# Four chained transformer layers on one core: Q, K and V made by feature and kept on chip, row terms by matmul, the order written out, GpSimd for the setup only

## The chip, the cores and the metric
The kernel runs on one core of a Trainium2 chip. The time is the device time of one launch in microseconds (us), median over runs. Engines: TensorE (PE, its weight loads PEld), VectorE (DVE), ScalarE (ACT), GpSimd (POOL), SyncE (SP, which here only issues transfers). All arithmetic is float32 unless stated; TensorE takes a float32 matmul in two passes, which are two instructions in the profile.

## What is computed
The input is x, 32 sequences of 32 tokens with 128 features. Four layers follow one another; each sequence has its own indices (expert 0 to 15, time step, expert 0 to 7), gate score and padding mask. Cut to what matters:

```python
# L0: adapter with a 32x32 expert matrix per sequence
h = gelu(x @ down_W.T + down_b);  h = h @ expert_W[d].T + expert_b[d] + domain_emb[d]
x = LN(h @ up_W.T + up_b + x) * ln_gamma + ln_beta
# L1: adaptive norm by time step, attention of 16 heads of 8 with bias and mask, FFN
scale, shift = split(silu(sin_emb(t)) @ W_ada + b_ada)
x = LN(x) * (1 + scale) + shift
x = x + softmax(q @ k.T / sqrt(8) + bias, masked) @ v @ Wo + bo
x = x + gelu2((LN(x) * g2 + beta2) @ W1 + b1) @ W2 + b2
# L2: FFN whose matrices (128x512, 512x128) are those of the sequence's expert
r = gelu(x @ Wi[e] + bi[e]) @ Wo[e] + bo[e] + x;  x = LN(r) * gamma[e] + beta[e]
# L3: causal attention and FFN on LN(x), then the gate
x = x + g * (layer(x) - x)
```

## The kernel before
**Tiles.** 32 x 32 tokens are 8 tiles of 128 rows (4 sequences each), tokens on the partitions. A tile goes through about 70 steps. Their names appear in the texts: `down`, `expert`, `up`, `res0` (L0); `stat_a`, `rstd_a`, `norm_a`, `aff_a` (its norm), the same with `_b` for the adaptive norm; `tr_b`, `ev_b` (transposition by TensorE and its eviction); `qkv1`, scores `sc1`, `mx1`, `sub1`, `exp1`, transposition of the probabilities `pt1`, `ctx1` (probabilities by V), `cn1` (division by the sum), `ct1`, output projection `wo1`, `res1`; FFN `ff1`, `act1`, `fo1`, `res2`; the expert layer `e1`, `et`, `gelu2`, `e2`, `res3`; L3's steps end in 3, and end with `ff3`, `act3`, `fo3`, `res5`, `gate`, `store`.

**Who does what.** TensorE (L549 to L684) does the products; it writes PSUM banks of 512 floats. VectorE (L764 to L944) takes most results out of PSUM and does statistics and norms. ScalarE (L687 to L761) does exp, gelu, the reciprocal roots (Ln then Exp on 128x1) and some evictions; it loads a function table (L730, L754, L760) at each change between the exp/ln and the gelu set. GpSimd (L947 to L1033) multiplies by gains, adds shifts and biases to the residual stream (`aff_a`, `aff_e`, `xbo*`, `xb2*`), and makes the block forms for the attention: `qbd` (Q with zeros outside its own sequence), `kex` (K, zeros outside its own head) and `vbd` (V). With these, four products of 128x128 per tile give all scores of 4 sequences and 16 heads (L633), on top of a product that puts the mask into the bank (L630).

**Q, K, V.** One product gives all three with tokens on the partitions (L622). VectorE adds the bias (L874) and transposes Q and K in 32x32 blocks (L879). V has to be on other partitions for `ctx`, so it goes to DRAM and is read back four times (L537, L541):

```python
sp.dma_start(vdram[k], qkv[:, k, 2 * D:3 * D])                       # vw
sp.dma_start(vrep[h * S:(h + 1) * S, k],
             vdram[k].rearrange("(b s) d -> s b d", b=NB))           # vr, 4 times
```

**Transfers.** All are issued by SyncE in one queue, in order: after the inputs, the attention bias `fs` (256 KB a tile), the modulation vector `ada` (each sequence's row spread over 32 partitions, L519), for each sequence its expert's matrices (512 KB, L530) and its rows of bias, gamma and beta (L532), V out and back. The weight ring has 5 tiles; a transfer waits for that of the same place in the tile before, so up to four are under way.

**Order.** A planner (`plan`) simulates the steps with durations written in a table (`STEPS`) and writes one fixed order for each engine, with buffers of 3 tiles (`SLOTS`) for nearly all that lies between the steps; an engine takes its instructions in that order and waits on semaphores.

## Time and profile before

| | us |
|---|---|
| median of 3 runs (183.81 to 186.43) | 184.84 |
| span of the profiled execution | 182.4 |
| lies around the span (median less span) | 2.4 |
| busy: TensorE, VectorE, ScalarE, GpSimd | 145.1, 132.3, 111.5, 89.2 |
| mean granted TensorE clock, share of 2.4 GHz | 0.878 |

The profiled execution has no time of its own beside its span, so the median stands for it. Busy time is the union of an engine's instructions; a matmul's shown length includes its way out of the array, so the distance from one start to the next is shorter than the length. "Issue" as the releaser of a wait means that the profile shows nothing that was waited for. PEclk is the granted clock: 1.0 is 2.4 GHz, 0.5 is 1.2 GHz, a mean lies between.

### The profile page before, as it was taken

What the parts mean: (1) busy time and instruction counts of PE and PEld (TensorE: products, weight loads), DVE (VectorE), ACT (ScalarE), POOL (GpSimd) and SP (SyncE); (2) the same over time, 40 slices, a digit from 0 to 9 for tenths busy, and PEclk for the clock granted to TensorE, in tenths of its full rate; (3) what the DMA queues carried; (4) which work ended last, traced back from release to release, by engine and by line L of the source; (5) the groups of instructions that cost most, each with busy time, mean ns of one, the idle gap of its engine ahead of it and who ended that gap; (6) DMA issues with size and microseconds to landing.
All of it is one profiled execution on the core that took longest, in us unless ns stands there. A gap on an engine that the chain in (4) does not pass through costs nothing.

```text
span 182.4 us, 4942 instructions
## 1 busy us (share of the span) xinstructions
PE 145.1 (80%) x1598; PEld 111.1 (61%) x1598; DVE 132.3 (73%) x400; ACT 111.5 (61%) x273; POOL 89.2 (49%) x137
## 2 busy tenths in 40 slices
PE   7999749470746749999899878866979899998884
PEld 7478525350534548976578648446646587887673
DVE  5847755461976869586758687896799999994823
ACT  2555644030141416949999889991484866979691
POOL 1112529280626698997323344329378577444300
PEclk9955555867597987999999999997999999999999
DMA  3996576426468389859768984997963222120101
GB/s 81 325 388 256 150 198 232 119 74 174 122 160 250 68 277 321 220 169 262 235 196 254 315 297 154 203 268 204 266 174 99 61 61 63 32 61 25 32 2 43
DMA packets 23848, 31.43 MB, mean 172 GB/s; under 512 B 3382, under 2 KB 18167, under 8 KB 23824
## 3 DMA queue, kind: packets, MB, share of 16 engines
q1 hardware_dynamic: 23554, 31.06, 57.6%
q8 instruction: 13, 0.21, 0.5%
q14 instruction: 11, 0.09, 0.2%
q10 hardware_dynamic: 270, 0.07, 0.2%
HBM read 28.50 MB, written 1.57 MB: 165 GB/s over the span
## 4 chain that ended last, share of the span: by engine, by line
SPq 36%; PE 21%; DVE 17%; issue 15%; ACT 4%; DMA 3%; POOL 1%; DVEq 0%; ACTq 0%
SPq L541 10%; SPq L532 9%; SPq L530 8%; SPq L529 5%; PE bank L633 4%; PE bank L659 3%; PE bank L664 3%; SPq L519 3%; DVE nrm L863 3%; PE bank L557 2%; DMA wexp<-in_wexp 2%; PE bank L622 2%; PE bank L671 2%; DVE xt L859 1%; DVE mx L897 1%
## 5 line engine op out<-in xcount | busy, mean ns | idle before, releaser
L732 ACT ACTIVATE lnv<-mv,eps 128x1 f32<-128x1 f32 x48 | 13.9, 290 | 18.4 <-DVE mv L854 18.1
L1011 POOL TENSOR_TENSOR vbd<-vrep,tab 128x512 f32<-128x512 f32 x16 | 17.4, 1090 | 14.9 <-DMA vrep<-vdram 10.6
L1003 POOL TENSOR_TENSOR qbd<-qkt,tab 128x512 f32<-128x512 f32 x16 | 17.6, 1104 | 11.9 <-DVE qkt L879 11.1
L633 PEld LDWEIGHTS bank<-kex,qbd 128*128 128x128 f32 x128 | 21.3, 236 | 1.6 <-issue 0.7
L633 PE MATMUL bank<-kex,qbd 128*128 128x128 f32 x128 | 21.0, 319 | 0.0
L659 PE MATMUL bank<-xt,tab 128*128 128x128 f32 x128 | 18.3, 289 | 1.5 <-DVE xt L859 1.2
L754 ACT ACTIVATE hg<-bank,tab 128x128 f32<-128x128 f32 x64 | 18.0, 383 | 1.7 <-PE bank L659 1.6
L622 PE MATMUL bank<-tab,xt 128*128 128x384 f32 x32 | 17.3, 638 | 1.9 <-DVE xt L859 0.9
L659 PEld LDWEIGHTS bank<-xt,tab 128*128 128x128 f32 x128 | 16.5, 200 | 3.9 <-issue 3.3
L664 PE MATMUL bank<-tab,hg 128*128 128x128 f32 x128 | 17.4, 281 | 1.5 <-ACT hg L754 1.4
L863 DVE TENSOR_SCALAR nrm<-res,mv,rstd 128x128 f32<-128x128 f32 x40 | 17.5, 446 | 1.2 <-ACT rstd L734 1.1
L664 PEld LDWEIGHTS bank<-tab,hg 128*128 128x128 f32 x128 | 15.4, 191 | 2.8 <-issue 2.6
L730 ACT ACT_TABLE_LOAD x12 | 15.4, 1283 | 2.7 <-DVE mv L854 2.5
L743 ACT ACTIVATE sc<-sc 128x512 f32<-128x512 f32 x16 | 10.0, 623 | 9.3 <-POOL sc L1018 8.4
L557 PE MATMUL bank<-tab,res 128*128 128x128 f32 x16 | 5.2, 327 | 12.8 <-DVE res L869 12.8
L737 ACT ACTIVATE xt<-bank 128x128 f32<-128x128 f32 x16 | 4.3, 271 | 17.4 <-PE bank L557 17.4
L746 ACT ACTIVATE pt<-bank 128x512 f32<-128x512 f32 x16 | 9.5, 597 | 6.6 <-PE bank L557 6.6
L874 DVE TENSOR_TENSOR qkv<-bank,rows 128x384 f32<-128x384 f32 x16 | 8.8, 552 | 6.4 <-issue 5.6
L1018 POOL TENSOR_TENSOR sc<-sc,mx 128x512 f32<-128x512 f32 x8 | 8.4, 1052 | 8.1 <-DVE mx L897 8.1
L557 PEld LDWEIGHTS bank<-tab,res 128*128 128x128 f32 x16 | 2.4, 151 | 16.1 <-issue 15.1
L557 PE MATMUL bank<-tab,sc 128*128 128x128 f32 x64 | 11.0, 300 | 1.4 <-ACT sc L743 1.2
L647 PE MATMUL bank<-vbd,pt 128*32 128x36 f32 x512 | 7.6, 201 | 5.5 <-POOL vbd L1011 5.4
(124 smaller groups left out, 348.2 us busy)
## 6 DMA issues: line engine op xcount, KB each, us to landing
wexp<-in_wexp SPq DMA_DIRECT2D x32, 512.0 KB, 4.1
vrep<-vdram SPq DMA_DIRECT2D x64, 64.0 KB, 3.0
fm<-in_fside SPq DMA_DIRECT2D x8, 256.0 KB, 4.9
tab<-in_tab SPq DMA_DIRECT2D x2, 768.0 KB, 7.9
selv<-in_eout SPq DMA_DIRECT2D x32, 48.0 KB, 4.7
adav<-emb SPq DMA_DIRECT2D x8, 128.0 KB
vdram<-qkv SPq DMA_DIRECT2D x16, 64.0 KB, 3.3
rows<-in_rows SPq DMA_DIRECT2D x1, 768.0 KB, 6.6
```

The lines of the kernel that those rows point to most:

```text
L532: sp.dma_start(selv[b * S:(b + 1) * S, t, :], a["eout2"][bass.ds(e, 1), :].broadcast_to([S, 3 * D])).then_inc(sig, 16)
L541: sp.dma_start(vrep[h * S:(h + 1) * S, k], vdram[k].rearrange("(b s) d -> s b d", b=NB)).then_inc(sig, 16)
L557: return pe.transpose(dst, src, ident)
L622: mm = pe.matmul(ps[:, 0:3 * D], xt[:, t, :], col("wqkv" + layer), start=True, stop=True)
L633: mm = pe.matmul(ps[:, g * P:(g + 1) * P], qbd[:, k, g].rearrange("p b s -> p (b s)"), kex[:, k, g].rearrange("p h s -> p (h s)"), start=F ...
L659: mm = pe.matmul(ps[:, c * P:(c + 1) * P], col("w1" + layer, c * P, P), xt[:, t, :], start=True, stop=True)
L664: mm = pe.matmul(ps[:, 0:D], hg[:, k, c, :], col("w2" + layer, c * D, D), start=(c == 0), stop=(c == C - 1))
L730: act.preload_act_table_set("natural_log_exp_and_others")
L754: ins = act.activation(hg[:, k, c, :], bank[BANK_OF["ff" + layer, t]][:, c * P:(c + 1) * P], ACT.Gelu_apprx_sigmoid if layer == "1" else A ...
L863: ins = dve.tensor_scalar(nrm[:, t, :], stream(layer, t), mv[:, t, 0:1], rstd[:, t:t + 1], ALU.subtract, ALU.mult)
L1003: ins = pool.tensor_tensor(qbd[:, k], qkt[:, k, 0, :, None, :].broadcast_to([P, HG, NB, S]), tab[:, None, at:at + NB, None].broadcast_to([ ...
L1011: ins = pool.tensor_tensor(vbd[:, k].rearrange("p b g w -> p (b g) w")[:, :, 0:H4 * DH].rearrange("p n (h d) -> p n h d", h=H4), vrep[:, k ...
```

## The change
**Tiles and grain.** Most steps take two tiles in one instruction or one group (statistics, norms, evictions, residual sums, FFN), the adapter four (its 32 features of four tiles lie on 128 partitions); Q/K/V, the scores and the expert products stay with one. `GRAIN` says which. Every tile has buffers of its own; the expert weights have a ring of 4 tiles in place of 5, with two transfers under way at once.

**Q, K, V by feature.** `q` and `kv` take the weights as the stationary operand, so Q and K come out with features on the partitions; Q's eviction by ScalarE scales and adds its bias (`qe`), K's by VectorE adds the bias and spreads it over four head masks (`kex`). V comes from 16 small products per tile, each 32 tokens by 32 features, put on the partitions where `vbd` needs it. V's bias is added behind `ctx` (`evct`), and K, V and the modulation vector are no longer transferred. The scores are 16 products of 32 rows by 32 columns of the array, over 4 PSUM banks.

**Row terms.** Bias rows, the modulation vector (`ada`) and the expert's bias, gamma and beta (`gb`, and rows in `e1`, `e2`) are added or made by a bf16 product of a table of ones (`oh3`, one 1 per sequence and term) with the rows split in three bf16 terms, so that their sum is the float32 row. GpSimd makes these tables once, VectorE that of the modulation vector. Norms with a gain are two VectorE instructions that read gain and shift where the product left them in PSUM (`normed`).

**Moved.** `aff_a`, `aff_e`, `sub1`, `kex1`, `vbd` from GpSimd to VectorE; the copy of `e1` to ScalarE; `xbo*`, `xb2*`, `norm_a`, `norm_b`, `norm_e`, `eb`, `qkvb`, `qkt`, `qbd` are gone; `res5` and `gate` become `base` (early) and `gate`.

**Order.** Five strings give each engine's order; TensorE's also gives the bank of each step. The planner is gone. The core of the diff (lines of before with -, of after with +):

```diff
-                    sp.dma_start(adav[:, k, :], for_tokens).then_inc(sig, 16)
...
-                    sp.dma_start(wexp[:, t % W_SLOTS, b, :],
-                                 a["wexp"][bass.ds(e, 1), :, :].rearrange("o p n -> (o p) n")).then_inc(sig, 16)
-                    sp.dma_start(selv[b * S:(b + 1) * S, t, :],
-                                 a["eout2"][bass.ds(e, 1), :].broadcast_to([S, 3 * D])).then_inc(sig, 16)
-                elif name in ("vw1", "vw3"):
-                    sp.wait_ge(done["qkvb" + layer], t + 1)
-                    sp.dma_start(vdram[k], qkv[:, k, 2 * D:3 * D]).then_inc(sig, 16)
-                elif name in ("vr1", "vr3"):
-                    arrived(sp, "vw" + layer, t)
-                    for h in range(H4):
-                        sp.dma_start(vrep[h * S:(h + 1) * S, k],
-                                     vdram[k].rearrange("(b s) d -> s b d", b=NB)).then_inc(sig, 16)
...
+                    if i >= 2:
+                        sp.wait_ge(wl_landed[i % 2], 16 * (i // 2))
+                    if t >= W_SLOTS and b == 0:
+                        ready(sp, "e2", t - W_SLOTS + 1)
+                    e = sp.value_load(eidx[0:1, i:i + 1], min_val=0, max_val=E2 - 1)
+                    sp.dma_start(wexp[:, t % W_SLOTS, b, :],
+                                 a["wexp"][bass.ds(e, 1), :, :].rearrange("o p n -> (o p) n")).then_inc(wl_landed[i % 2], 16)
+                    if not late:
+                        late = True
+                        sp.dma_start(tab[:, t3:NCOL], a["tab"][:, t3:NCOL]).then_inc(loaded["tab3"], 16)
...
-                    mm = pe.matmul(ps[:, 0:3 * D], xt[:, t, :], col("wqkv" + layer), start=True, stop=True)
...
-                    pe.matmul(ps[:].rearrange("p (h s) -> p h s", h=H), ident_bf[:],
-                              masked[:, None, :].broadcast_to([P, H, S]), start=True, stop=False)
-                    for g in range(HG):
-                        mm = pe.matmul(ps[:, g * P:(g + 1) * P], qbd[:, k, g].rearrange("p b s -> p (b s)"),
-                                       kex[:, k, g].rearrange("p h s -> p (h s)"), start=False, stop=(g == HG - 1))
...
+            def add_rows(dst, t, table, lo, n, start=False):
+                return pe.matmul(dst, oh3[:, t].rearrange("k b s -> k (b s)"), table[:, lo:lo + n],
+                                 start=start, stop=False)
...
+                    pe.matmul(dst[:, 0:P], col("wqkv" + layer, D, D), xt[:, i, :], start=True, stop=True)
+                    wv = col("wqkv" + layer, 2 * D, D).rearrange("p (g h d) -> p g h d", g=HG, h=H4)
+                    for b in range(NB):
+                        for h in range(H4):
+                            mm = pe.matmul(dst[h * S:(h + 1) * S, P + b * HG * DH:P + (b + 1) * HG * DH],
+                                           xt[:, i, b * S:(b + 1) * S], wv[:, :, h, :], start=True, stop=True,
+                                           tile_position=(0, h * S))
...
+                    for g in range(HG):
+                        pe.matmul(ps[:, at + g, 0:P].rearrange("p (h s) -> p h s", h=H4), ident_bf[:],
+                                  masked[:, None, :].broadcast_to([P, H4, S]), start=True, stop=False)
+                    for b in range(NB):
+                        for g in range(HG):
+                            part = slice(g * S, (g + 1) * S)
+                            mm = pe.matmul(ps[b * S:(b + 1) * S, at + g, 0:P], qt[part, i, b * S:(b + 1) * S],
+                                           kex[part, i, :, b * S:(b + 1) * S], start=False, stop=True,
+                                           tile_position=(g * S, b * S))
...
-                    link(dve.tensor_tensor(res[:, t, :], nrm[:, t, :], adav[:, k, 0:D], ALU.mult))
-                    ins = dve.tensor_tensor(res[:, t, :], res[:, t, :], adav[:, k, D:2 * D], ALU.add)
...
-                    ins = dve.tensor_tensor(qkv[:, k, :], bank[BANK_OF["qkv" + layer, t]][:, 0:3 * D],
-                                            row("bqkv" + layer, 3 * D), ALU.add)
...
-                    ins = dve.transpose(qkt[:, k].rearrange("p j g s -> p (j g s)"), qkv[:, k, 0:2 * D])
...
+            def normed(layer, i, gain, shift):
+                ts = tiles_of("aff_" + layer, i)
+                ready(dve, "rstd_" + layer, ts[-1] + 1)
+                for n, t in enumerate(ts):
+                    ins = dve.scalar_tensor_tensor(nrm[:, t, :], res[:, t, :], mv[:, t, 0:1], gain(n), ALU.subtract,
+                                                   ALU.mult)
+                link(ins)
+                for n, t in enumerate(ts):
+                    ins = dve.scalar_tensor_tensor(res[:, t, :], nrm[:, t, :], rstd[:, t:t + 1], shift(n), ALU.mult,
+                                                   ALU.add)
+                return ins
...
+                    ins = dve.scalar_tensor_tensor(
+                        kex[:, i], bank("kv" + layer, i, P)[:, None, :].broadcast_to([P, H4, P]), bqk[:, n, 1:2],
+                        col("head_mask")[:, :, None].broadcast_to([P, H4, P]), ALU.add, ALU.mult)
...
+                    ins = dve.tensor_tensor(
+                        vbd[:, i].rearrange("p b g w -> p (b g) w")[:, :, 0:H4 * DH].rearrange("p n (h d) -> p n h d", h=H4),
+                        bank("kv" + layer, i)[:, P:2 * P].rearrange("p (n d) -> p n d", n=n)[:, :, None, :].broadcast_to(
+                            [P, n, H4, DH]),
+                        col("seq_mask")[:, None, :, None].broadcast_to([P, n, H4, DH]), ALU.mult)
...
-                    ins = dve.scalar_tensor_tensor(nrm[:, t, :], resb[:, t, :], gate[:, t:t + 1], x_in[:, t, :],
-                                                   ALU.mult, ALU.add)
...
+                        ins = dve.scalar_tensor_tensor(x_in[:, t, :], bank("wo3", i)[:, n * D:(n + 1) * D], gate[:, t:t + 1],
+                                                       res[:, t, :], ALU.mult, ALU.add)
...
+                        ins = dve.scalar_tensor_tensor(res[:, t, :], bank("fo3", i)[:, n * D:(n + 1) * D], gate[:, t:t + 1],
+                                                       x_in[:, t, :], ALU.mult, ALU.add)
...
+                    ins = act.activation(qt[:, i, :], bank("q" + layer, i, P), ACT.Identity, bias=bqs[:, n:n + 1],
+                                         scale=1.0 / math.sqrt(DH))
...
-                    link(pool.tensor_tensor(res[:, t, :], nrm[:, t, :], selv[:, t, D:2 * D], ALU.mult))
-                    ins = pool.tensor_tensor(x_in[:, t, :], res[:, t, :], selv[:, t, 2 * D:3 * D], ALU.add)
...
-                    ins = pool.tensor_tensor(qbd[:, k], qkt[:, k, 0, :, None, :].broadcast_to([P, HG, NB, S]),
-                                             tab[:, None, at:at + NB, None].broadcast_to([P, HG, NB, S]), ALU.mult)
...
-                    ins = pool.tensor_tensor(sc[:, k], sc[:, k], mx[:, t, :, None].broadcast_to([P, H, S]),
-                                             ALU.subtract)
...
+PE_ORDER = """
+w_selb.0@0 w_sel.0@2 down.0@1 down.1@4 w_emb.0@5 expert.0@6 expert.1@7 w_bi.0@2 up.0@4 up.1@0 ada.0@4 ada.1@5
...
```

In the following pieces the rows are an engine's instructions in their built order, output<-inputs and shape, with the program's buffer names (`bank` and `ps` are PSUM, `xt` the transposed tile, `tab` the table of weights).

SyncE before, from the second tile's V on its way out to the first tile's on its way back (`adav` is the modulation vector, `selv` the expert's rows, `fm` the attention bias):

```order
L537 DMA vdram<-qkv 128x128
L519 DMA adav<-emb 128x1x256
L537 DMA vdram<-qkv 128x128
L529 TENSOR_LOAD eidx
L529 ISA x2
L530 ISA
L530 DMA wexp<-in_wexp 128x1024
L532 ISA
L532 DMA selv<-in_eout 32x384
L521 DMA fm<-in_fside 128x512
L541 DMA vrep<-vdram 32x4x128 x4
```

SyncE after, from the attention bias on; TENSOR_LOAD to the weights is one sequence, 31 more follow, and behind them the stores alone:

```order
L360 DMA sc<-in_fside 128x512 x8
L370 TENSOR_LOAD eidx
L370 ISA x2
L371 ISA
L371 DMA wexp<-in_wexp 128x1024
L375 DMA tab<-in_tab 128x1536
L370 TENSOR_LOAD eidx
```

Between V's way out and its way back stand further weights, rows and the modulation vector; afterwards only the weights follow one another.

TensorE before, up to the first `ctx1` (L557 transpositions, L622 Q/K/V of a tile, L630 mask, L633 scores, L647 `ctx1`):

```order
L630 MATMUL bank<-mask_neg,ident_bf 128x512
L633 MATMUL bank<-kex,qbd 128x128 x4
L622 MATMUL bank<-tab,xt 128x384
L557 MATMUL bank<-tab,sc 128x128 x4
L630 MATMUL bank<-mask_neg,ident_bf 128x512
L633 MATMUL bank<-kex,qbd 128x128 x4
L557 MATMUL bank<-tab,res 128x128
L647 MATMUL bank<-vbd,pt 32x36 x16
```

TensorE after, around the first `ctx1` (L497 mask, L502 scores, L508 transposition of the probabilities, L457 `ada`, L470 and L523 transpositions, L517 `ctx1`, L480 K, L485 V of a tile):

```order
L502 MATMUL ps<-kex,qt 32x128 x16
L508 MATMUL ps<-tab,sc 128x128 x4
L457 MATMUL ps<-emb,oh 128x256 x2
L497 MATMUL ps<-mask_neg,ident_bf 128x128 x4
L502 MATMUL ps<-kex,qt 32x128 x16
L508 MATMUL ps<-tab,sc 128x128 x4
L470 MATMUL ps<-tab,res 128x128 x2
L517 MATMUL ps<-vbd,pt 32x36 x32
L480 MATMUL ps<-xt,tab 128x128
L485 MATMUL ps<-tab,xt 32x32 x16
L508 MATMUL ps<-tab,sc 128x128 x4
L523 MATMUL ps<-tab,qt 128x128 x2
```

The first `ctx1` is one of two tiles, stands behind both tiles' transposed probabilities, and has no transfer ahead of it; a score group is 16 small products, and K and V of a later tile are 1 and 16.

VectorE before, around the first adaptive norms (L863 norm, L868 and L869 modulation, L874 Q/K/V bias, L879 transposition of Q and K):

```order
L868 TENSOR_TENSOR res<-nrm,adav 128x128
L869 TENSOR_TENSOR res<-res,adav 128x128
L863 TENSOR_SCALAR nrm<-res,mv,rstd 128x128
L850 TENSOR_TENSOR res<-bank,x_in 128x128
L868 TENSOR_TENSOR res<-nrm,adav 128x128
L869 TENSOR_TENSOR res<-res,adav 128x128
L874 TENSOR_TENSOR qkv<-bank,rows 128x384
L853 BN_STATS bn<-res 128x6
L854 BN_AGGR mv<-bn 128x2
L879 STREAM_TRANSPOSE qkt<-qkv 128x256
```

VectorE after, around the first adaptive norms and the first K and V (L687 and L691 norm with gain and shift, L803 K's block form, L810 V's, L825 and L832 the scores' bias and maximum):

```order
L687 SCALAR_TENSOR_TENSOR nrm<-res,mv,ps 128x128 x2
L691 SCALAR_TENSOR_TENSOR res<-nrm,rstd,ps 128x128 x2
L687 SCALAR_TENSOR_TENSOR nrm<-res,mv,rows 128x128 x2
L691 SCALAR_TENSOR_TENSOR res<-nrm,rstd,rows 128x128 x2
L803 SCALAR_TENSOR_TENSOR kex<-ps,bqk,tab 128x512
L810 TENSOR_TENSOR vbd<-ps,tab 128x16x32
L803 SCALAR_TENSOR_TENSOR kex<-ps,bqk,tab 128x512
L810 TENSOR_TENSOR vbd<-ps,tab 128x16x32
L825 TENSOR_TENSOR sc<-ps,sc 128x512
L803 SCALAR_TENSOR_TENSOR kex<-ps,bqk,tab 128x512
L832 TENSOR_REDUCE mx<-sc 128x16
```

The norms of two tiles stand together and read their gains from `ps`; K's and V's forms, made by GpSimd before, stand between them and the scores.

## Rows read from the trace of the kernel before

**Rows 1.** The page, part 1: busy us (share of the span) xinstructions.
```profile
PE 145.1 (80%) x1598; PEld 111.1 (61%) x1598; DVE 132.3 (73%) x400; ACT 111.5 (61%) x273; POOL 89.2 (49%) x137
```

**Rows 2.** Windows: us, busy us of each engine, PEclk, DMA share, GB/s.
```profile
21.00:56.30 35.30, 19.12 (x70) 12.81 (x71) 20.36 (x57) 10.39 (x29) 16.80 (x24) 0.69 0.56 160
56.30:163.80 107.50, 93.41 (x1234) 72.01 (x1235) 88.21 (x247) 78.32 (x184) 63.90 (x92) 0.95 0.64 186
163.80:182.40 18.60, 13.80 (x157) 11.62 (x155) 9.13 (x33) 12.09 (x34) 3.76 (x7) 1.00 0.09 27
...
140.00:160.00 20.00, 18.87 (x272) 14.72 (x271) 19.46 (x60) 15.06 (x39) 13.09 (x21) 1.00 0.21 59
```

**Rows 3.** Waits: who for whom, us, times, longest (first two from 21.0 to 56.3).
```profile
PE bank L557 <- DVE res L869: 12.1, 4, 6.7
...
DVE res L868 <- DMA adav<-emb: 6.9, 3, 4.1
...
PE bank L647 <- POOL vbd L1011: 5.4, 2, 3.5
```

**Rows 4.** Timeline of SyncE's queue: start us, us, queue, line, transfer.
```profile
37.66 0.52 SPq L537 DMA_DIRECT2D vdram<-qkv  x1
...
46.32 3.46 SPq L532 DMA_DIRECT2D selv<-in_eout  x1
...
50.30 1.85 SPq L541 DMA_DIRECT2D vrep<-vdram  x4
```

**Rows 5.** Timeline of TensorE, two places at the 2.4 GHz level.
```profile
61.30 0.88 PE L622 MATMUL bank<-tab,xt 128*128 128x384 f32 x2
62.02 0.38 PE L630 MATMUL bank<-mask_neg,ident_bf 128*128 128x512 bf16 x1
62.23 1.05 PE L633 MATMUL bank<-kex,qbd 128*128 128x128 f32 x8
63.12 0.27 PE L557 MATMUL bank<-tab,cx 128*128 128x128 f32 x1
63.23 0.27 PE L557 MATMUL bank<-tab,nrm 128*128 128x128 f32 x1
65.42 0.47 PE L647 MATMUL bank<-vbd,pt 128*32 128x36 f32 x32 [1.92 <-POOL vbd L1011]
65.82 0.38 PE L655 MATMUL bank<-tab,cxt 128*128 128x128 f32 x1
...
103.60 1.08 PE L681 MATMUL bank<-wexp,hg 128*32 128x128 f32 x32
104.50 1.04 PE L671 MATMUL bank<-wexp,xt 128*32 128x512 f32 x8
105.35 1.06 PE L681 MATMUL bank<-wexp,hg 128*32 128x128 f32 x32
```

**Rows 6.** VectorE's groups (busy us, mean ns; second: ns min/median/max).
```profile
L863 DVE TENSOR_SCALAR nrm<-res,mv,rstd 128x128 f32<-128x128 f32 x40 | 17.5, 446 | 1.2 <-ACT rstd L734 1.1
...
L874 DVE TENSOR_TENSOR qkv<-bank,rows 128x384 f32<-128x384 f32 x16 | 8.8, 552 | 6.4 <-issue 5.6 <-PE bank L622 0.8
...
L863 DVE TENSOR_SCALAR nrm<-res,mv,rstd x40: 304/340/1080, 16.0 to 174.0; 128x128 f32<-128x128 f32 x40
```

**Rows 7.** Timeline of ScalarE, a table load.
```profile
103.71 1.28 ACT L730 ACT_TABLE_LOAD   x1
105.01 0.29 ACT L732 ACTIVATE lnv<-mv,eps 128x1 f32<-128x1 f32 x1
```

**Rows 8.** Timeline of VectorE: first res0, last sub3, last gate.
```profile
13.04 0.29 DVE L850 TENSOR_TENSOR res<-bank,x_in 128x128 f32<-128x128 f32 x1 [0.44 <-PE bank L609]
...
163.77 0.69 DVE L889 TENSOR_TENSOR sc<-bank,mx 128x512 f32<-128x512 f32 x1
...
180.07 0.35 DVE L942 SCALAR_TENSOR_TENSOR nrm<-resb,gate,x_in 128x128 f32<-128x128 f32 x1
```

**Rows 9.** Line L530, the expert weights.
```profile
DMA to landing us min/median/max: 3.3/4.1/8.1
```

1192 lines of the change are left out of this document (544 added, 648 removed), and 4 rows, old and new, of the table DRAIN.

## The prediction
> **What bounds the kernel now.** I read the page's shares first. TensorE is busy 80% of the span, VectorE 73%, ScalarE 61%, GpSimd 49% [rows 1]: no engine is full, and four take part in each tile's chain. The stretches come next [rows 2]. From 21.0 us (the first transposition of a tile) to 56.3 us (the first product of probabilities with V) TensorE is busy 19.1 of 35.3 us and VectorE 20.4, and the granted clock is 0.69, so most of these matmuls ran at 1.2 GHz. From 56.3 to 163.8 us TensorE is busy 93.4 of 107.5 us and VectorE 88.2, clock 0.95. The last 18.6 us are one chain.
>
> The list of waits says what the poor stretch waited for: TensorE 12.1 us for `aff_b`'s result on VectorE, and VectorE in turn 6.9 us for the transfer of the modulation vector [rows 3]. The queue shows why. SyncE issues all these transfers in one row with the expert weights; one issue of an expert's rows holds it for 3.46 us, and the first V, sent out at 37.66, is asked back only at 50.30, 12.6 us later [rows 4]. So the first 56 us are bound by SyncE's queue, the 107 us after by TensorE and VectorE together.
>
> **What the change makes of the queue.** V is made by product straight into the layout that the block form needs, the modulation vector and an expert's rows become products with a table of ones: SyncE keeps the loads, the expert weights and the stores, none of which has to wait for a result except a weight's ring slot. All of GpSimd's work per tile goes too, and with it the GpSimd links of the chain.
>
> **TensorE, step by step, at 2.4 GHz.** I take the pitch, start to start, since a matmul's shown length contains its tail. From [rows 5]: Q, K and V at once 0.72 us; the mask 0.21; the four score products 0.89 (8 passes of 128 columns, 0.11 each, which is also the price of the hidden layers' four products); the 32 column-tiled passes of `ctx` 0.40; the 32 of `e2` 0.90; the 8 of `e1` 0.85; one transposition 0.11. A tile has Q/K/V and scores twice: 16 x 0.72 = 11.5, scores with mask 16 x 1.10 = 17.6, 152 transpositions 16.7, `ctx` 16 x 0.40 = 6.4, hidden layers 32 x 0.89 = 28.5, output projections 16 x 0.22 = 3.5, `e1` and `e2` 8 x 1.75 = 14.0. Sum 98.2 us.
>
> After: Q and K are two 0.22 products, V is 32 column-tiled passes like `ctx`: 0.84 in place of 0.72, +1.9. The rows added by product are 40 of 128 columns, 8 of 512 and 16 of 256 in bf16; at the mask's 0.21 for 512 that is +5.5. The scores are now 32 small passes in place of 8 large. No row of this kernel shows the new form (32 rows by 32 columns at 16 places). The low end is the 0.40 of `ctx`'s 32 passes, the high end 32 x 0.11 = 3.5 if they run one by one; I take the 0.90 of `e2`, which has 128 columns too: +0.2. Sum 106 us. Of it 10.5 us lie in the last chain (9 hidden groups, 2 `ctx`, 1 group of transpositions, 3 projections, 6 single ones), so 95.5 us are for the middle.
>
> **VectorE.** The means times counts of all its groups (the costliest two kinds stand in [rows 6]; the other figures here are from the same table) make 150 us before, the page says 132.3 [rows 1]: instructions overlap, the factor is 0.88. Changes: the Q/K/V bias and the 32x32 transposition of Q/K go (8.8 + 7.0); K's block form goes from 8 on VectorE to 16 at some 0.70 and V's form comes, 16 at 0.68, +16; `sub1` comes, 8 x 0.68, +5.4; the copy of `e1` goes to ScalarE and the expert bias to a product, -11.0. The 48 normalisations at 0.446 and the modulation (0.382 + 0.484) become 24 at 0.34 and 48 two-step ones at 0.35 (`gate`'s length undisturbed [rows 8]): -3.4, and aff_a and aff_e of GpSimd are in it. Pairs of tiles in one instruction (evictions 24 x 0.40 to 12 x 0.53, residual sums, `cn`): -10.6. The rest (base, gate, setup) is +1.2. Sum: 132, times 0.88 = 116 us busy.
>
> The 0.34 is the undisturbed length: beside a GpSimd instruction the same normalisation takes up to 1.08 us, and its mean is 0.446 against a median of 0.34 [rows 6]. GpSimd's setup (about 13 us by its own rates, over by some 25 us) may still hold a few instructions of the start by up to 1 us each.
>
> **ScalarE.** 31 table loads become 23, -10.3; 48 pairs of `rstd` become 24, -11.8; hidden activations in 256 columns, -5.5; Q's eviction +4.6, `e1`'s copy +4.8, the rest -3.1: 111.5 to 90. It bounds nothing. A table load costs 1.28 us and the next instruction starts 0.02 us behind its end [rows 7]. The Trainium skill (ScalarE: Activation LUTs, What ACT_TABLE_LOAD costs) gives about 2.66 us a switch, with a drain behind the load. By that the 8 fewer would be worth 21 us of ScalarE; these rows show no drain, so my sum has 10.3, and as ScalarE is covered either way the time is the same.
>
> **The sum.** Start: `res0` of tile 0 begins at 13.04 now [rows 8]; afterwards `up` has four tiles and stands behind a table product that needs a late load, so I put 14.5. VectorE then has 8.5 us of work in its new order up to the first `aff_b` of two tiles: first transposition at 23 (21.0 now). End: the last `sub3` to the last `gate` takes 180.4 - 163.8 = 16.6 us [rows 8] and keeps its links: 16.6 again.
>
> Middle: between 56.3 and 163.8 the kernel before did 98.2 - 9.8 (done earlier) - 10.5 = 77.9 us of pitch work in 107.5, a density of 0.725. Of the missing 29.6, 5.4 us are TensorE's wait for GpSimd's V [rows 3], about 5 the time at 1.2 GHz (clock 0.95), 14 in all are idle, the rest tails of single matmuls before a wait. Without GpSimd's wait, half the clock's and a third of the tails (groups now hold two tiles) some 19 us would stay on 77.9: 0.80 to 0.82. I take 0.82: 95.5 / 0.82 = 116.5. VectorE has 116 less 8 (setup), 8.5 (up to `aff_b`) and 8.5 (the last chain) = 91 us in the same stretch, 78%: it fits beside, and is the second bound. Span 23 + 116.5 + 16.6 = 156.1 us. The profiled span is 182.4 and the median of the three runs 184.84, 2.4 us lie around it: 158.5. So the forecast is 158 us.
>
> Both ends: at the old density, 95.5 / 0.725 = 131.7, the time is 173.7. At 0.93, which is where VectorE's 91 us fill 98% of the middle (it reached 19.46 of 20 us from 140 to 160 [rows 2]), 102.7 and the time is 144.7. The scores' low end takes 16 x 0.5 / 0.82 = 10 us off TensorE's part.
>
> **Rivals.**
> 1. Dense middle, 147 us. For it: 8 tiles' buffers instead of rings of 3, no transfer in the chain. Against: two engines of almost equal work, each in a fixed order, wait for each other.
> 2. Density as before, 173 us. For it: the order is fixed and written for durations that the chip may not keep; the early part ran at 1.2 GHz for lack of work and may again.
> 3. The weights decide, 172 us. The ring has 4 slots in place of 5, and two transfers are under way at once where there were up to four. The first `e2` stands at a third of TensorE's work, about 64 us, and tile 4's weights start there. At 4.1 us each [rows 9] a tile takes 8.2 and tile 7 is there at 97, before its turn at about 112. At the slowest landing seen, 8.1, it comes at 129, and the end some 14 us later than forecast. Against: V's, the modulation's and the experts' rows' transfers, which share the 16 engines with the weights now, are gone.
> 4. Slower, 209 us: the small score products run one by one. 3.5 us in place of 0.90, 16 times, is +42 on TensorE: 137 / 0.82 = 167, span 207. It decides from about +1.35 us a group on (21.5 us in all). For it: four in a row have the same 32 output partitions, and only the four column places are seen overlapping in this trace ([rows 5]: 32 x 0.11 would be 3.5, `e2` takes 0.90). Against: each of the four writes a bank of its own.
>
> Rival 4 has a page beside it. The Trainium skill (TensorEngine Tiling (Array Packing), Gotcha 1: PSUM Pressure) says different row tiles cannot use one PSUM bank at the same time; the four banks meet it, no run shows it. The same page (Key Properties) says that a change of tiling mode drains the array, which speaks against this change, as V and the scores add some 64 changes. In this trace a full product starts 0.07 us before the shown end of `ctx`, so no drain is seen [rows 5]; were each change to wait out a pass's tail, 0.16 us (the scores are shown 1.05 long at a pitch of 0.89), that would be 10 us of TensorE and 12 of time, inside the range.
>
> That the change doesn't do what it says is excluded by the built order: GpSimd has 17 instructions after the constants, none in a tile's chain.
>
> **Chances.** Forecast (density 0.77 to 0.87, 152 to 167 us) 0.48; rival 1 0.22; rival 2 0.13; rival 3 0.05; rival 4 0.07; no gain because stalls of several kinds add up to the old time 0.05. A measurement of this kernel tells about 2% from no change. Faster by over 2%: 0.88; within 2%: 0.05; slower: 0.07. The range 141 to 177 leaves out rival 4, the case without gain and a little of the dense end.
>
> **What would show it.** Right: the first `ctx` before 40 us in place of 56.3; TensorE idle under 15 us between the first transposition and the last `sub3`; VectorE near 116 us busy with the `norm` form at 0.34; 32 score passes within 1.1 us; the last chain 15 to 18 us. Wrong: score groups over 2 us (rival 4); waits of `e1` for the weights (rival 3); a granted clock under 0.8 past 40 us or waits of TensorE and VectorE for each other over 25 us (rival 2).

## The result: faster by 2.9%, 21 us short of the forecast

The changed kernel takes 179.44 us in the median of four runs (179.01 to 180.01), the kernel before 184.71 on the same chip: ratio 0.971, 95% interval 0.965 to 0.977. The forecast was 158 us, its range 141 to 177. The profiled execution took 179.0 us with a span of 176.3. Executions of one kernel lie 1 to 7 us apart, and those of e3_pool, e6_vact, e8_mask2 and e9_tail2 that were profiled are slow ones, more than 1.5% above the fastest of the same kernel.

### The profile after

The page's first part and, of the second, the rows of TensorE, VectorE and the granted clock (tenths in 40 slices of 4.4 us):

```profile
span 176.3 us, 6271 instructions
PE 138.0 (78%) x2582; PEld 101.3 (57%) x2582; DVE 118.7 (67%) x340; ACT 93.9 (53%) x188; POOL 15.5 (9%) x22
...
PE   7919800198786499999987889999999869776893
...
DVE  3625469978998979074965697638846998645611
...
PEclk9999999999999879999999999999999999996699
```

The busy times are those forecast: VectorE 118.7 (116 forecast), ScalarE 93.9 (90), GpSimd 15.5. TensorE is busy for less time than before ([rows 1]: 145.1) and the span is shorter by only 6 us. Windows cut at the first transposition of a tile, at the first hidden layer `ff1` and at the last `sub3` show where the time is:

```profile
core 0: us, PE busy (x) PEld busy (x) DVE busy (x) ACT busy (x) POOL busy (x), PEclk, DMA share, GB/s
0.00:34.16 34.16, 16.95 (x162) 10.11 (x163) 20.22 (x69) 9.68 (x19) 15.52 (x22) 1.00 0.81 247
34.16:61.41 27.25, 20.22 (x532) 15.06 (x533) 24.50 (x66) 10.55 (x27) 0.00 (x0) 0.99 0.69 211
61.41:152.90 91.49, 83.66 (x1672) 62.09 (x1672) 64.64 (x176) 65.47 (x124) 0.00 (x0) 0.99 0.33 96
152.90:176.30 23.40, 17.14 (x219) 14.06 (x218) 9.32 (x31) 8.20 (x19) 0.00 (x0) 0.85 0.06 18
```

The start is 34.2 us, where 23 were forecast and 21.0 stood before. From there to 61.4 us VectorE is the fuller engine (24.5 of 27.3 us, TensorE 20.2). From 61.4 to 152.9 us it is TensorE (83.7 of 91.5), VectorE has 65. Against [rows 2] the program has two parts that differ in their fullest engine.

The clock of 1.00 in the first row is not to be trusted. The trace of this execution has clock records only from 40.2 us on, and the view counts what lies before them as full speed. The products say otherwise: the four passes of `w_sel` take 3.78 us here and 1.98 in e4_start, whose trace has a recorded clock of 1.00 at that place.

```profile
5.28 3.78 PE L403 MATMUL ps<-pt,oh 17*128 17x512 f32 x4
```
```profile
4.85 1.98 PE L403 MATMUL ps<-pt,oh 17*128 17x512 f32 x4
```

The two passes of K likewise take 0.77 us at 35.4 us and 0.49 at 40.4. So this execution too was at 1.2 GHz up to 40 us, and its mean clock (0.97) stands too high.

What the start waits for stands in the list of waits:

```profile
engine line waited for: us in total, times, longest us
...
POOL bqs L901 <- DMA bqk<-in_rows: 11.9, 1, 11.9
PE ps L470 <- DVE res L691: 11.7, 1, 11.7
...
ACT xt L642 <- PE ps L523: 7.3, 6, 2.8
DVE res L867 <- PE ps L542: 7.1, 4, 4.2
DVE sc L825 <- PE ps L502: 6.7, 4, 4.4
```

TensorE's 11.7 us before its first transposition are again a wait for `aff_b`. The 12.1 us in [rows 3] lay behind the first transposition, these lie ahead of it. The waits for the modulation's transfer and for GpSimd's V, the other two of that group, are gone. GpSimd's first setup step sits 11.9 us behind two transfers of 1 KB, the Q and K biases. The timeline of GpSimd (POOL) and VectorE (DVE) shows what follows. Columns: start us, us, engine, line, operation.

```profile
12.81 0.23 POOL L901 TENSOR_SCALAR bqs<-bqk 128x2 f32<-128x2 f32 x1 [11.89 <-DMA bqk<-in_rows]
...
20.03 1.14 POOL L886 TENSOR_TENSOR brow<-kex,brow 32x512 bf16<-32x512 f32 x1
...
22.55 1.26 POOL L907 TENSOR_TENSOR x_in<-x_in,rows 128x512 f32<-128x512 f32 x1
...
24.77 1.87 POOL L884 TENSOR_TENSOR erow<-erow,ex 64x896 f32<-64x896 f32 x1
...
27.70 1.87 POOL L886 TENSOR_TENSOR ex<-erow,ex 32x896 bf16<-32x896 f32 x1
```
```profile
20.11 0.69 DVE L765 TENSOR_TENSOR res<-ps,x_in 128x512 f32<-128x512 f32 x1 [2.20 <-PE ps L451]
...
23.92 0.69 DVE L765 TENSOR_TENSOR res<-ps,x_in 128x512 f32<-128x512 f32 x1 [1.66 <-POOL x_in L907]
24.53 2.26 DVE L687 SCALAR_TENSOR_TENSOR nrm<-res,mv,rows 128x128 f32<-128x128 f32 x2
26.82 2.90 DVE L691 SCALAR_TENSOR_TENSOR res<-nrm,rstd,rows 128x128 f32<-128x128 f32 x2
29.65 0.60 DVE L687 SCALAR_TENSOR_TENSOR nrm<-res,mv,rows 128x128 f32<-128x128 f32 x2
```

Three losses: the first `res0` comes at 20.11 us in place of 14.5; the second waits 1.66 us for GpSimd's `xub.1`, which stood behind row tables and masks; and two pairs of VectorE take 2.26 and 2.90 us where the next pair takes 0.60, for just as long as GpSimd makes the row table `ex3`. That is 5.6 + 1.7 + 4.0 = 11.3 us, as much as the whole excess. e4_start below, without the second and the third, takes 9.2 us from the first `res0` to the first transposition, where this kernel takes 14.1 and 8.5 were forecast.

TensorE about 65 us, at the full clock, with the new score form (L502) in it:

```profile
64.67 0.39 PE L497 MATMUL ps<-mask_neg,ident_bf 128*128 128x128 bf16 x4
64.98 0.50 PE L502 MATMUL ps<-kex,qt 32*32 32x128 f32 x32
65.41 0.49 PE L480 MATMUL ps<-xt,tab 128*128 128x128 f32 x2
```

32 score passes take 0.43 us of pitch (64.98 to 65.41), where I took 0.90, with full products right before and behind. The four mask passes ahead of them take 0.31. In e8_mask2, which has eight, they take 0.55, so four more cost 0.24, and some 0.09 of the 0.31 belong to the change from full to small products.

```profile
88.59 0.62 PE L497 MATMUL ps<-mask_neg,ident_bf 128*128 128x128 bf16 x8
89.14 0.50 PE L502 MATMUL ps<-kex,qt 32*32 32x128 f32 x32
```

### The profile page after: what moved, and what is told of

It is laid out like the page before. It is cut to its first block, busy times and chain, and to the rows that moved or that the text cites. A ratio compares the mean times of both kernels' runs of the same rounds, so it can differ in the third digit from the quotient of the medians.

```text
span 176.3 us, 6271 instructions
## 1 busy us (share of the span) xinstructions
PE 138.0 (78%) x2582; PEld 101.3 (57%) x2582; DVE 118.7 (67%) x340; ACT 93.9 (53%) x188; POOL 15.5 (9%) x22
## 4 chain that ended last, share of the span: by engine, by line
PE 51%; DVE 21%; issue 7%; ACT 7%; SPq 5%; DMA 4%; POOL 3%; DVEq 0%; POOLq 0%
PE ps L534 9%; PE ps L542 8%; PE ps L561 5%; DMA kex<-in_rows 4%; PE ps L550 4%; PE ps L390 3%; PE ps L485 3%; DVE nrm L687 3%; DVE bn L770 3%; DVE res L691 3%; PE ps L480 2%; PE ps L508 2%; PE ps L470 2%; PE ps L529 2%; PE ps L475 2%
## 5 line engine op out<-in xcount | busy, mean ns | idle before, releaser
L534 PE MATMUL ps<-xt,tab 128*128 128x256 f32 x64 | 18.4, 439 | 1.6 <-DVE xt L787 1.3
L620 ACT ACTIVATE lnv<-mv,eps 128x2 f32<-128x2 f32 x24 | 7.0, 293 | 22.6 <-DVE mv L773 22.3
L542 PE MATMUL ps<-tab,pt 128*128 128x128 f32 x128 | 16.8, 281 | 0.0
L534 PEld LDWEIGHTS ps<-xt,tab 128*128 128x128 f32 x64 | 13.7, 225 | 4.2 <-issue 2.2
L542 PEld LDWEIGHTS ps<-tab,pt 128*128 128x128 f32 x128 | 15.6, 192 | 0.2
L803 DVE SCALAR_TENSOR_TENSOR kex<-ps,bqk,tab 128x512 f32<-128x512 f32 x16 | 11.9, 745 | 3.3 <-PE ps L485 3.3
L649 ACT ACTIVATE pt<-ps,tab 128x256 f32<-128x256 f32 x32 | 12.5, 477 | 1.5 <-PE ps L534 1.3
L470 PE MATMUL ps<-tab,res 128*128 128x128 f32 x16 | 3.7, 320 | 11.7 <-DVE res L691 11.7
L639 ACT ACTIVATE pt<-ps 128x512 f32<-128x512 f32 x16 | 9.4, 594 | 4.2 <-PE ps L508 4.1
L810 DVE TENSOR_TENSOR vbd<-ps,tab 128x512 f32<-128x512 f32 x16 | 10.7, 678 | 0.3 <-PE ps L485 0.3
L508 PE MATMUL ps<-tab,sc 128*128 128x128 f32 x64 | 9.6, 278 | 0.5 <-ACT sc L636 0.5
L825 DVE TENSOR_TENSOR sc<-ps,sc 128x512 f32<-128x512 f32 x8 | 5.5, 683 | 6.7 <-PE ps L502 6.7
L485 PE MATMUL ps<-tab,xt 128*32 128x32 f32 x512 | 8.2, 204 | 1.8 <-issue 1.8
L770 DVE BATCH_NORM_STATS2 bn<-res 128x6 f32<-128x128 f32 x40 | 9.5, 279 | 0.2
L470 PEld LDWEIGHTS ps<-tab,res 128*128 128x128 f32 x16 | 2.1, 160 | 12.9 <-issue 12.6
L480 PE MATMUL ps<-xt,tab 128*128 128x128 f32 x32 | 7.6, 321 | 2.2 <-DVE xt L787 1.6
```

The costliest lines, as they stand in the source:

```text
L480: pe.matmul(dst[:, 0:P], col("wqkv" + layer, D, D), xt[:, i, :], start=True, stop=True)
L485: mm = pe.matmul(dst[h * S:(h + 1) * S, P + b * HG * DH:P + (b + 1) * HG * DH], xt[:, i, b * S:(b + 1) * S], wv[:, :, h, :], start=True, s ...
L508: mm = pe.transpose(dst[:, g * P:(g + 1) * P], sc[:, i, g * H4:(g + 1) * H4, :].rearrange("p h s -> p (h s)"), ident)
L534: mm = pe.matmul(ps[:, BANK_OF[name, i] + c // 2, (c % 2) * 2 * P:(c % 2 + 1) * 2 * P], col("w1" + layer, c * P, P), tok, start=True, stop ...
L542: mm = pe.matmul(y, hg[:, i, c, n * P:(n + 1) * P], col("w2" + layer, c * D, D), start=False, stop=(c == C - 1))
L649: ins = act.activation(hg[:, i, c, :], ps[:, at + c // 2, (c % 2) * 2 * P:(c % 2 + 1) * 2 * P], ACT.Gelu_apprx_sigmoid if layer == "1" els ...
```

## The experiments

Times are medians of 4 runs or more. Seven runs of the kernel before stand beside each; they have medians of 184.0 to 185.9 us. Places in the table are of the profiled execution of each kernel: first transposition of a tile, first `ff1`, first `e1`, last `sub3`, and from there to the end of the last `gate`.

| kernel | transp. | ff1 | e1 | last sub3 | last chain | time |
|---|---|---|---|---|---|---|
| changed | 34.2 | 61.4 | 73.3 | 152.9 | 21.2 | 179.4 |
| e12_again | 33.4 | 60.3 | 72.6 | 155.5 | 20.9 | 179.8 |
| e1_wbis | 30.5 | 62.3 | 74.3 | 153.1 | 20.6 | 180.2 |
| e2_xt | 35.5 | 64.1 | 75.7 | 155.3 | 21.0 | 180.8 |
| e3_pool | 34.8 | 63.9 | 75.9 | 156.8 | 20.2 | 180.5 |
| e4_start | 30.0 | 60.8 | 73.3 | 153.7 | 20.9 | 178.5 |
| e5_start2 | 27.3 | 55.7 | 70.0 | 153.0 | 20.3 | 177.7 |
| e10_warm | 35.4 | 63.2 | 75.3 | 155.5 | 19.8 | 178.9 |
| e18_late | 27.9 | 56.2 | 70.5 | 150.4 | 19.8 | 174.1 |
| e17_early | 27.6 | 54.8 | 67.5 | 147.0 | 21.4 | 171.7 |
| e14_comb | 28.0 | 54.1 | 66.8 | 146.1 | 19.8 | 170.5 |
| e13_comb | 27.4 | 52.7 | 65.4 | 146.1 | 19.5 | 170.3 |

changed and e12_again are one kernel. Their last `sub3` lie 2.6 us apart, so a smaller difference between two rows tells nothing until the traces show where it comes from.

### One cause of the start at a time

**e1_wbis**, GpSimd's operations on `ex3` held back:

```diff
 elif name == "w_bis":
     ready(pool, "w_bic", 1)
+    ready(pool, "sub1", 4)
```

> The edit: GpSimd's four operations on ex3 (24.77 to 29.57 us in the changed kernel) wait until the fourth sub1 is done, about 50 us; nothing is left out. Theory S (the start is long by stalls that add up, and what follows is TensorE work that shifts with it): VectorE's two pairs at 24.53 and 26.82 (2.26 and 2.90 us) take 0.60 each, the first transposition of a tile comes at 30.2 instead of 34.2 us, and the time falls by about 4 us, to 175.5 (ratio to the kernel before 0.950). Rival M (the time is set in the middle or by the weights, and the start is absorbed): the transposition comes earlier, but the last sub3 stays at 153 us and the time at 179. Rival X (the two slow pairs are not due to GpSimd): both the pairs and the time stay as they are. If GpSimd's operations then hold VectorE's between 50 and 60 us, up to 4 us come back there.

Measured: 180.21 us, ratio to the kernel before 0.979 (0.969 to 0.988). The hold is GpSimd's: where it no longer runs the pairs take 0.60 us, and it holds VectorE again where it runs now.

```profile
24.76 0.60 DVE L687 SCALAR_TENSOR_TENSOR nrm<-res,mv,rows 128x128 f32<-128x128 f32 x2
25.40 0.61 DVE L691 SCALAR_TENSOR_TENSOR res<-nrm,rstd,rows 128x128 f32<-128x128 f32 x2
...
51.19 3.02 DVE L687 SCALAR_TENSOR_TENSOR nrm<-res,mv,rows 128x128 f32<-128x128 f32 x2
54.25 2.18 DVE L691 SCALAR_TENSOR_TENSOR res<-nrm,rstd,rows 128x128 f32<-128x128 f32 x2
```
```profile
51.19 1.89 POOL L884 TENSOR_TENSOR erow<-erow,ex 64x896 f32<-64x896 f32 x1
53.14 0.92 POOL L885 CAST ex<-erow 64x896 bf16<-64x896 f32 x1
54.14 1.87 POOL L886 TENSOR_TENSOR ex<-erow,ex 32x896 bf16<-32x896 f32 x1
```

Rival X is out. The transposition came 3.7 us earlier, as theory S has it, and the last `sub3` stayed at 153.1, as rival M has it. That does not decide for M: the two pairs at 51 us take 5.2 us in place of 1.2, so the 4.0 us came back there, and TensorE is at a granted clock of 0.50 from 55.0 to 65.2 us, where the changed kernel is for 3.4 us.

**e2_xt**, the second half of `xt` requested earlier:

```diff
 sp.dma_start(xt[:, 0:4]...)
+sp.dma_start(xt[:, 4:NT]...)
 sp.dma_start(x_in[:], ...)
```

> The edit: the transfer of the second half of xt is issued right behind the first, ahead of x, rows and the ada table. The second down product then no longer waits 3.8 us to 13.43. Theory S with the start's legs in parallel: w_emb's sum on VectorE comes some 2 us earlier (from 15.2 to 13), the first res0 moves from 20.1 to 18, but the second res0 still waits for GpSimd's xub.1 (22.55, 1.26) and the two slow pairs stay, so the first transposition stays within 0.5 us of 34.2 and the time within 1 us of 179.4. If xt_rest alone decides the start, the transposition comes at 31 and the time is 176.

Measured: 180.82 us (0.981, 0.974 to 0.987). No gain, and not for my reason alone: `w_emb`'s sum on VectorE came at 16.7 us, not at 13, since the table it needs now arrives later. GpSimd's wait for `bqk` grew too, from 11.9 to 13.3 us. Here the loads share one pace, and what is put ahead delays the rest.

**e3_pool**, GpSimd's order "w_adb w_oh3 xub.0 xub.1 w_bqs w_pre w_rows w_neg w_bis", with `w_bqs` the scaling that waits for `bqk`.

> The edit: on GpSimd the scaling of the Q bias, which waits for bqk to 12.81 us, is a step of its own behind both xub, and xub.1 comes ahead of the row tables and the masks. Theory S: xub.1 is done before 15 us, the second res0 comes at 22.3 instead of 23.92, VectorE's idle time of 1.66 us goes, and the first transposition comes 1.7 us earlier, at 32.5, the time 1 to 2 us lower, 178. If more of the start hung on that queue (w_emb's sum waits for GpSimd's ada_b), up to 3 us. Rival M: the transposition moves, the time does not.

Measured: 180.50 us (0.972, 0.962 to 0.982). The second `res0` follows the first with no wait, but the first came at 22.0 us (20.1): the one wait became another, as a cast on VectorE (L750, 0.33 us before) took 1.81 us beside the two `xub`.

**e4_start**, these three together, with `w_emb` and `w_bi` moved on TensorE.

> The three edits together, and on TensorE the product w_emb ahead of the second down and w_bi (four passes that took 3.5 us) behind both up; the copy of w_bi's result on ScalarE behind the second rstd_a. Theory S: the stalls add: the first res0 at 16.5 (20.1), no wait for xub.1, pairs of 0.60, so the first transposition at 25 us instead of 34.2; the middle stays 118 us, the last sub3 comes at 144 and the time is 170.5 us (ratio to the kernel before 0.923). Rival M: the last sub3 at 150 or later and the time 176 or more, since the weights (e2.0 frees the first slot) or VectorE between 25 and 60 take up the gain.

Measured: 178.54 us (0.968, 0.961 to 0.975). The transposition at 30.0, not 25, since the transfers set it: TensorE's `w_emb` waits 8.7 us for its table, to 15.9. Of these 4.2 us nothing is left at the last `sub3` against the row of the changed kernel, and 1.8 against that of e12_again. Again two pairs of VectorE are held at 51 us (3.8 us for 1.2), and the clock is 0.50 from 55.4 to 65.5 us.

**e5_start2**, the start written anew; the new heads of the orders:

```diff
 PE_ORDER = """
-w_selb.0@0 w_sel.0@2 down.0@1 down.1@4 w_emb.0@5 expert.0@6 expert.1@7 w_bi.0@2 up.0@4 up.1@0 ada.0@4
+w_selb.0@0 w_sel.0@2 down.0@1 expert.0@6 up.0@4 down.1@0 expert.1@1 up.1@0 w_emb.0@4 w_bi.0@6 ada.0@4
 DVE_ORDER = """
-w_oh0.0 w_ang.0 w_sbc.0 w_oh2.0 w_selc.0 w_embc.0 ebias.0 ebias.1 res0.0 stat_a.0 stat_a.1 res0.1 aff_a.0
+w_oh0.0 w_ang.0 w_sbc.0 w_oh2.0 w_selc.0 ebias.0 res0.0 stat_a.0 stat_a.1 ebias.1 res0.1 w_embc.0 aff_a.0
```

> The edit: the start written so that no leg waits for another. TensorE does the first unit's down, expert and up before the second unit's, then w_emb and w_bi; VectorE does the first res0 and its statistics before the second ebias, and w_embc behind the second res0; GpSimd does both xub first and the Q bias apart; ex3's casts go to ScalarE and its two differences to VectorE between 60 and 70 us, where VectorE has waits, instead of to GpSimd. Theory D (VectorE bounds the program up to about 61 us, TensorE from there): in the two runs with a shorter start the first ff1 came at 60.8 and 62.3 us whatever the start, since VectorE was held again by GpSimd at 50 us (3.8 us instead of 1.2). Without that hold the first transposition comes at 26 us and the first ff1 at 54 instead of 61.4, and the time is 173 (ratio 0.940). Theory C (the granted clock gives it back: a TensorE that waits more falls to half clock, and ff1 then takes 3.6 instead of 2 us): the first ff1 at 55 to 57, the last sub3 at 150 and the time at 177.

Measured: 177.72 us (175.57 to 178.44), no interval. Here the start's gain does reach the first `ff1` (5.7 us earlier); at the first `e1` 3.3 us of it are left, and at the last `sub3` nothing against the changed kernel. A part is lost at 95 to 100 us:

```profile
90.00:95.00 5.00, 3.29 (x76) 2.75 (x75) 2.79 (x6) 4.01 (x7) 0.00 (x0) 0.92 0.60 200
95.00:100.00 5.00, 4.70 (x15) 3.80 (x15) 2.83 (x10) 2.97 (x5) 0.00 (x0) 0.50 0.62 179
```

TensorE is busy 4.70 of 5 us with 15 instructions, at a granted clock of 0.50: the 1.2 GHz level in the densest part of the program. The hidden layer there takes 3.75 us in place of 1.97. TensorE had waited 1.71 us from 92.1 on, in the middle of a V group, for nothing that the profile shows:

```profile
93.81 0.44 PE L485 MATMUL ps<-tab,xt 128*32 128x32 f32 x26 [1.71 <-issue]
```

But the trace of e12_again, the unaltered kernel, has the same fall at 98 us: from the first `e1` to the last `sub3` it takes 82.9 us and e5_start2 83.0, where the changed kernel takes 79.6. The fall costs some 3 us and does not come with the short start. Against e12_again the 6.1 us of the start are 4.6 at the first `ff1`, 2.6 at the first `e1` and 2.4 at the last `sub3`. What is lost is lost ahead of the first `e1`, where e5_start2 is at a clock of 0.50 for 6.8 us (53.3 to 60.1) and e12_again for 3.4.

### What bounds the two halves

**e8_mask2** doubles the mask passes of the scores. **e11_norows** leaves the row products out, and with them the biases. The edit of e8_mask2, cut:

```diff
-for g in range(HG):
-    pe.matmul(... ident_bf ... start=True, stop=False)
+for g in range(2 * HG):
+    pe.matmul(... ident_bf ... start=True, stop=g < HG)
```

> The edit: each of the 64 bf16 mask passes of the scores is done twice (the second starts the sum anew, the result is the same): 64 passes more, 0.08 us each. Theory D: the last twelve score steps lie where TensorE bounds (past 60 us), so the last sub3 comes 12 x 4 x 0.08 = 3.7 us later and the time is 183; the four before cost little. Rival (TensorE has as much slack as its idle time, or the end hangs on VectorE or the weights): under 1.5 us, time 180.5.

> Left out: the row products of wo1, wo3, fo1, fo3, e1 and e2, that is all biases that the change adds by products there (48 passes, 32 with 0.06 us of pitch by 128 columns, 8 of 0.3, 8 of 0.07). Theory D (past 61 us TensorE bounds, and its work shifts the end one for one): 40 of the 48 lie past 61 us, 4.7 us in all, so the last sub3 comes 4 us earlier and the time is 175. Rival (the end hangs on VectorE, ScalarE or the weights): under 1.5 us.

Measured: 182.38 us (181.04 to 185.89) and 175.33 us (174.22 to 179.07; ratio 0.954, 0.937 to 0.970). From the first `ff1` to the last `sub3` it is 94.6 us with 48 passes more and 88.2 without the rows, against 91.5: +3.1 (3.7 expected) and -3.3 (4 expected). The expected sizes were too high. At the pitch in these traces e8_mask2's 48 passes are 2.7 us (0.056 each). The 35 row products of that stretch are 4.9 us, of which 16 are the last full product ahead of small ones; the 0.09 us for that change stays without them, so some 3.4 us go (my estimate from these rows). changed, e1_wbis, e2_xt, e7_tail and e10_warm, with the same work there and no fall of the clock in its midst, take 90.7 to 92.3 us, so both runs lie outside. The waits agree: past 61 us VectorE waits 21.9 us for TensorE, and TensorE 3.7 for VectorE. So there TensorE's work is the time, about one for one. The profiled execution of e8_mask2 is the longest of its four (185.9 us; the others 181.0 to 183.0). The other 5 us of its later end came ahead of `ff1` (66.6), with a granted clock of 0.66 and 0.80 from 55 to 65 us.

**e16_nosub** takes VectorE's work away in the first half:

> Left out: the eight mx1 and sub1 (the first attention's maximum and its subtraction), 1.2 us a tile on VectorE; its softmax is then taken without the maximum. Theory D (VectorE bounds from 34 to 61 us): the first four tiles' 4.8 us come off, the first ff1 at 57 to 58 instead of 61; past it TensorE bounds and the other four tiles bring nothing: the time 3 to 4 us lower, 176. Rival (the chain of one tile or TensorE bounds there): the first ff1 at 60 or later, time 179.

Measured: 180.27 us, but 176.2 to 182.6 over four runs, no interval. In the profiled execution the first `ff1` began at 59.4 from a transposition at 33.6: 25.8 us in place of 27.3. 1.1 to 1.5 of the 4.8 us came through, as e12_again has 26.9; once these eight operations are gone VectorE waits for TensorE in turn (1.16 us before `res1`). That is nearer to the rival (59.4 us; 57 to 58 under theory D, 60 or later under the rival): VectorE is the fullest engine there, but it isn't shown to be the limit. In the changed kernel's stretch VectorE waits 2.4 us for TensorE and TensorE 3.4 for VectorE. The time stays open.

**e6_vact** sends `vbd1` to ScalarE, four operations of 0.28 us each a tile:

> The edit: the eight vbd1 (0.60 us each on VectorE) go to ScalarE, four operations each with the sequence mask as scale, in the part where ScalarE is busy for 10 of 26 us. Theory D: from 34 to 60 us VectorE is what bounds (23.1 busy of 25.8), so four to six of them taken away there (2.4 to 3.6 us) bring the first ff1 from 61.4 to 58.5 us, and the time to 176.5. Rival: TensorE or ScalarE's chain decides there too, or the mask operations on ScalarE take over 1.2 us a tile and sit ahead of qe1 and exp1: no change or 1 us slower.

Measured: 183.25 us (181.72 to 185.19), slower than the unaltered kernel on the same chip (178.81 to 181.08). VectorE's relief brought nothing: ScalarE's 1.13 us per tile sit ahead of `exp1` (first one at 46.9 us, 44.0 in the changed kernel), and in the profiled execution, the longest of five, the first `ff1` slipped to 67.2 us. A moved operation counts by its place in the chain.

### The last chain

**e7_tail** and **e9_tail2** reorder it; e9_tail2's TensorE order ends with `wo3.3` ahead of `tr_g.2`:

```diff
-sc3.7@4 fo3.1@0 ctx3.2@2 pt3.6@3 pt3.7@1 ct3.2@4 wo3.2@5 ctx3.3@6 ct3.3@7 tr_g.2@0 wo3.3@2 ff3.2@4
+sc3.7@4 ctx3.2@2 fo3.1@0 pt3.6@3 pt3.7@1 ct3.2@4 wo3.2@5 ctx3.3@6 ct3.3@7 wo3.3@2 tr_g.2@0 ff3.2@4
```

> The edit: in the last chain TensorE does the third ctx3 and the last two pt3 around fo3.1, the fourth ctx3 before wo3.2, and VectorE the last cn3 before base.2 and stat_g.2 (it stood 1.7 us behind them). Theory T (the last chain is 21.2 us instead of 16.6 by its order): from the last sub3 to the end 18.5 to 19, time 177. Rival (it is 21.2 since ff3.2 runs at half clock, 3.6 instead of 2.0 us, and two tile pairs end together): 20.5 to 21, time 179.

> The edit: the last chain again, with what the first attempt showed: the fourth wo3 no longer stands behind the third tr_g (which waited 2.0 us for norm_g), the last cn3 comes before base.2, the last res4 and its statistics before ev_g.2, and the last evct3 ahead of rstd_g.2. Theory T (order): 18.5 us from the last sub3 to the last gate instead of 20.6, time 177.5. Theory C (ff3.2 at half clock, 3.6 instead of 2.0 us, is the larger part): 20 us, time 179.

Measured: 180.43 us (179.86 to 186.57) and 181.42 us (178.57 to 183.09; 0.975, 0.960 to 0.991), last chain 22.6 and 21.5 us. Theory T falls: the chain did not get shorter. `ff3.2` took 3.62 and 3.65 us, at half clock in both.

### The granted clock

**e12_again** is the unaltered kernel, **e10_warm** adds products of zeros where TensorE waits:

```diff
+for _ in range(FILL.get((name, i), 0)):
+    pe.matmul(dst[:, 0:P], idle_bf[:], idle_bf[:], start=True, stop=True)
```

> The changed kernel unaltered, on the same chip as the three that follow, so that differences of 1 to 2 us can be read against it. Expected 179.4 us, within 1 us. Theory C says that its granted clock differs from one execution to the next (0.865 to 0.971 so far) with little change of the time, since TensorE at half clock before 35 us waits for VectorE anyway, and that only a fall past 50 us costs.

> The edit: 196 bf16 products of zeros (0.08 to 0.11 us each) on TensorE in front of the steps that it waited for (30 before the second down, 90 before the first tr_b, 51 at seven places from 41 to 60 us, 42 at six places of the last chain), written into the bank that the step uses next. Theory C (waits bring the half clock, and the half clock costs what ff1.0 and ff3.2 show, 3.6 instead of 2.0 us each): the clock stays full through 55 to 66 and 160 to 167 us, and the time falls by 2 to 4 us, to 176. Rival: the falls come back elsewhere in the dense part or the fillers delay the steps behind them: within 1 us of the unaltered kernel, or slower.

Measured: 179.81 us (0.976, 0.965 to 0.987) and 178.89 us (0.972, 0.961 to 0.983). The clock of e10_warm is 1.00 in every stretch from 45 to 170 us and the last chain is 1.1 us shorter; the whole is 0.9 us better, below what two such medians can tell. e12_again's four executions took 179.5, 180.1 and 181.1 us at a mean clock of 0.875 to 0.885 and 178.8 at 0.981. That is no measure of what half clock ahead of 35 us costs: the changed kernel's trace, with a mean of 0.97, was at half clock there too, as its products showed. The next four kernels put fillers onto the short start. The first two have 183 and 186 fillers, from 22 us on, and differ in the last chain, in its order and its fillers:

> The edit: the start written anew (as in the run of that name), the last chain reordered, and fillers on TensorE only at the waits from 22 us on and in the last chain (more of them there). Theory D with C (start, dense part and last chain add once the clock does not fall): first ff1 at 55.7, dense part 91.5, so the last sub3 at 147.5; last chain 18 us; span 167, time 170 us (ratio 0.92). Rival (the program's middle has a length of its own, set by VectorE or the weights): last sub3 at 151 or later, time 175 or more.

> The same without the reordered last chain. Last sub3 at 147.5, last chain 19.2 us as in the run with fillers, time 171.5 us. If the reordered chain is worth nothing, the two runs agree within 0.5 us.

Measured: **170.29 us** (169.66 to 171.58), ratio 0.926 (0.917 to 0.934), and 170.51 us, 0.927 (0.919 to 0.934). The page of e13_comb:

```profile
PE 145.7 (87%) x2765; PEld 108.4 (65%) x2765; DVE 118.1 (70%) x342; ACT 95.3 (57%) x190; POOL 10.3 (6%) x18
...
PEclk9999999999999999999999999999999999999999
```

The clock records of this trace begin at 27.2 us; ahead of that its four `w_sel` passes take 3.78 us, so the row is right from the seventh slice on.

The last chain gave 19.5 us, not the 18 expected, and as much without its new order (19.8): that order is worth nothing. Against e10_warm, with fillers as well, e14_comb has its transposition 7.4 us earlier, its last `sub3` 9.4 us and its median 8.4 us: with fillers the start counts one for one or better. Which fillers do it:

> The shortened start with fillers at eight waits from 22 to 56 us only (109 products of zeros). Theory C (a TensorE that waits in that stretch loses the full clock at about 50 to 60 us, and once more some 35 to 40 us later, in the dense part): no half clock from 45 us up to the last chain, the last sub3 at 146 to 147 us, the last chain 20.5 us, time 172. Rival (those of the last chain bring it): the last sub3 at 150 or later, time 176.

> The shortened start with fillers at six waits of the last chain only. Theory C: half clock at about 55 us and in most executions once more between 90 and 105, the last sub3 at 150 to 153, the last chain 19.3 us, time 176. Rival: the last sub3 at 147 and the time 171.

Measured: 171.65 us (0.925, 0.916 to 0.934) and 174.06 us (0.935, 0.921 to 0.949). The early ones carry most of it. The windows of e17_early over its first half, its dense part and its last chain:

```profile
27.62:54.82 27.20, 24.35 (x611) 19.33 (x612) 24.15 (x66) 10.55 (x27) 0.00 (x0) 0.88 0.70 209
54.82:146.96 92.14, 82.82 (x1673) 60.97 (x1672) 66.84 (x179) 66.07 (x125) 0.00 (x0) 1.00 0.35 112
146.96:170.60 23.64, 17.26 (x219) 14.13 (x217) 9.33 (x31) 8.19 (x19) 0.00 (x0) 0.86 0.06 17
```

Its dense part, first `ff1` to last `sub3`, is 92.1 us at clock 1.00. e18_late takes 94.2, and its first 4.6 us are at half clock:

```profile
54.00:60.80 6.80, 6.19 (x38) 4.71 (x53) 5.76 (x15) 1.45 (x5) 0.00 (x0) 0.50 0.65 196
60.80:150.40 89.60, 81.24 (x1673) 60.05 (x1666) 62.81 (x167) 65.48 (x122) 0.00 (x0) 1.00 0.33 103
```

So what the early fillers take away is the half clock about the first `ff1`. Every profiled execution without them falls to it between 46 and 63 us, for 3.4 us or more; the four with them are at the full clock from 42 us at the latest to 153 us. Without early fillers 2.4 to 2.5 us of a start's gain arrive at the last `sub3` (e5_start2 against e12_again, of 6.1; e18_late against the changed kernel, of 6.3), with them 5.9 of 6.5 (e17_early against the changed kernel) and 9.4 of 7.4 (e14_comb against e10_warm).

The full clock also matters ahead of `ff1`. e13_comb, e14_comb and e17_early have the same orders and fillers there. They come back to 2.4 GHz at 27.2, 32.7 and 34.4 us, and take 25.3, 26.1 and 27.2 us from the transposition to `ff1`. So TensorE is a limit in this part too.

The fall in the dense part is another matter. e18_late has no early fillers and no such fall, so nothing shows that the early fillers prevent it. In e5_start2 and e12_again it came behind the wait of 1.71 us in kv3.1 (at 92 and 95 us); in the changed kernel that wait was 1.17 us, in e18_late 0.61, and the clock stayed. The two other waits of TensorE of over 1.5 us between 70 and 140 us (e15_vdram aside) were followed by a fall as well: 2.22 us in e9_tail2 (at 126.6 us, for an expert's weights) and 2.95 us in the kernel before (at 121.8). A wait of 1.44 us at 135 to 150 us, which 17 of the traces have, was followed by one in e3_pool and e4_start alone. These are executions side by side, no experiment on the wait, so the cause is likely and not shown.

### V through DRAM again

**e15_vdram**: one V product, a copy by VectorE, then on GpSimd's queue

```diff
+pool.dma_start(a["vdram"][t], vst[:, t]).then_inc(vs_landed, 16)
+pool.wait_ge(vs_landed, 16 * (n + 1))
+for h in range(H4):
+    pool.dma_start(vrep[h * S:(h + 1) * S, t % 4], a["vdram"][t]...)
```

> The edit on the changed kernel: V is one product again, VectorE copies it out of PSUM (16 copies more), GpSimd's queue stores it and loads it back four times, and vbd is made from there, seven places later on VectorE. TensorE's V passes cost 0.2 us less per tile (16 x 0.2 = 3.2 us), VectorE has 16 x 0.25 = 4 us more. My forecast's reason (the on-chip V takes 8 us of waits out of each tile's chain, so density rises from 0.725): the first ctx3 and ctx1 come 5 us later, the dense part is 5 us or more longer, time 186 or more. Rival (with eight tiles' buffers and this order the trip is hidden, as the written order gives it time): 179 to 181 us, and the gain of the middle is from the other parts.

Measured: 210.81 us (207.26 to 213.36), ratio 1.133 (1.116 to 1.149).

```profile
POOL vrep L941 <- DMA vdram<-vst: 40.9, 16, 4.8
DVE vbd L810 <- DMA vrep<-vdram: 23.2, 9, 5.6
...
PE ps L497 <- DVE sc L827: 13.2, 1, 13.2
```

A trip takes 11 us (copy at 37.1, block form at 48.4), the queue does one at a time, every 6 to 7 us, and the fixed orders let it all through: 31 us. That is more than my 5 or more and rules out that the written order hides it. It is the price of this trip on this queue, which does one at a time; the kernel before's trip had another queue, so the run doesn't measure what V on chip brought.

## Why the forecast missed

The profiled execution is 20.5 us above the 158.5 of the sum. The terms: start +11.2, middle +2.2, last chain +4.6, end +2.2, around the span +0.3.

**The start failed (23 us; 34.2).** Three steps of it. "`res0` of tile 0 at 14.5" took the table's transfer as the late one; it came at 20.1, behind the second `xt` and `w_bi`, which stand ahead of the first `up` in TensorE's order, and the modulation's sum, which stands ahead of `ebias` in VectorE's. The order's rows showed that queue and I priced one member of it. "GpSimd's setup may still hold a few instructions of the start by up to 1 us each" was the right mechanism, priced by its single instruction; it was never put into the sum, and four in a row cost 4.0 us. And GpSimd's wait for two transfers of 1 KB had no term at all. e5_start2, written against these three, has its first `res0` at 13.65 us and the transposition at 27.3.

**The middle came out right (116.5; 118.7) by two errors.** The 32 score passes cost 0.43 us, not 0.90: 7.5 us less; the mask 0.31, not 0.21: 1.6 more, nearly all of it the change to small products. With 89.6 us of pitch in 118.7 the density is 0.755, not 0.82; that of the kernel before was 0.725. So density did stay nearly as it was, rival 2's mechanism, without its time. Its sign of waits came too: between the first transposition and the last `sub3` TensorE and VectorE wait 31.4 us for each other (VectorE 24.3, TensorE 7.1), and over 25 was to mean rival 2. Its sign of a clock under 0.8 past 40 us came only for 3.4 us at 61 us and 6.8 at 160. One density over the whole middle is the wrong model: for 91.5 us TensorE is the bound, which e8_mask2 and e11_norows show, and for the 27 us before neither engine alone is shown to be. The high end of the density was also mis-worked: 91 us of VectorE in 102.7 are 89%, not 98%.

**The last chain failed ("keeps its links", 16.6; 21.2).** With the clock kept up it is 19.5 to 19.8, so 1.1 to 1.7 us of the 20.9 and 21.2 of the unaltered kernel are the half clock. The other 3 us are as I read the rows, two pairs of tiles side by side: `ff3`, `act3` and `fo3` for four tiles stand in it. No run isolates that, and none made it shorter by order.

**The end** is a slip: the sum ran to the last `gate` and added only what lies around the span, and left out the 2.0 us from there to the span's end.

What held: VectorE's and ScalarE's busy times; `norm` at 0.34 us (0.341); TensorE idle 14.9 us between the first transposition and the last `sub3` (under 15); scores far below 2 us, so no rival 4; no wait of `e1` for weights, so no rival 3, though next to no weights moved from 65 to 80 us, the ring being full. The first `ctx` at 49.2 us instead of before 40 was the sign of the late start.

The Trainium skill (TensorEngine Tiling (Array Packing), Key Properties) says that a change of tiling mode drains the array. The prediction saw no drain in the trace of before, since the next product starts ahead of the shown end. The pitch is the better sign. It shows a cost of the change, which agrees with the page, though no run tells a drain from another cost: the last full pass ahead of small ones takes some 0.09 us more than its like (mask passes 0.056 apart, 0.149 to the first score pass), and the first full pass starts 0.20 us behind the last score pass, 0.13 behind V's last. Over the 16 score and 16 V groups that is some 7 us of TensorE, an estimate from these rows; the prediction priced it at 10 at most and left it out of the sum.

**Shown and not shown.** Shown: that GpSimd holds VectorE, that past 61 us TensorE bounds, that the start's gain arrives in full where fillers keep the clock up ahead of the first `ff1` and by under half where they don't. Not shown: which of the change's parts brought the 24 us that the middle got shorter; e15_vdram says only that V's trip, put into this order on GpSimd's queue, would cost more than the whole gain. Also open: what TensorE waits for in kv3.1, and what bounds the 27 us ahead of `ff1`. Not tried: a version with less of VectorE's work in the first half and its chain unharmed.

## What to carry to other kernels

Cut the program where the fullest engine changes, and price each part by itself. Where two engines are both nearly full, relief of one brings only a share (1.1 to 1.5 of 4.8 us here). A late start must be traced through every in-order queue that it passes (loads, GpSimd, TensorE), since each takes the place of the last as soon as one is mended. And before an edit is called worthless, compare executions with like falls of the clock: e5_start2 seemed to keep nothing of its start beside an execution without a fall in the dense part, and kept 2.4 us beside one with it. With 109 products of zeros in the waits ahead of the dense part the same start kept nearly all.

## What the runs showed of the chip

- VectorE's operations with two inputs in SBUF stand still while a GpSimd `TENSOR_TENSOR` runs: 2.26 to 3.02 us for a pair of 0.60. A cast from SBUF to SBUF is held too (e3_pool: 1.81 us in place of 0.33). A sum with one input in PSUM (0.69 at 20.11, beside L886) and statistics aren't. The Trainium skill (SBUF — State Buffer, SBUF: two separate sides) says that GpSimd and a VectorE operation with two SBUF inputs, or in a two-port mode, lock a shared pair of ports against each other; the traces agree.
- 32 passes of 32 rows by 32 columns and 128 wide, spread over 16 places and four banks, take 0.43 us up to the next full product, of which 0.20 are the last pass and the change back; two full passes take 0.24 (66.50 to 66.74). The change from full to small products costs 0.09 us.
- TensorE fell to half clock in the middle of its densest part, with 4.53 of 5 us busy just before (85 to 90 us) and one wait of 1.71 us (e5_start2). It costs 1.8 us a hidden layer (3.75 against 1.97 us).
- A product of zeros at the full clock costs 0.06 us of pitch.
- Two 1 KB transfers of single elements landed 8.0 us after issue, later than the two loads of `xt` with 256 KB each (6.0 us).
- A trace's clock records can begin late (40.2 us in the changed kernel's); the view shows full clock ahead of them, while products there take twice as long.
